# AdaLN layer on one core: the first norm's modulation as columns, three x buffers, one routed sum z per tile, and a new order

## The reference

```python
mod = (silu(c) @ wmod).reshape(4, 6, 1, 256)
sa, ca, ga, sb, cb, gb = mod[:, 0], ..., mod[:, 5]     # ga, gb: sign * max(|.|, 0.25)
h = layernorm(x) * (1 + ca) + sa
x = x + ga * attn(h)        # 16 query heads in 4 groups, d 16, rope, causal softmax over 1024
h = layernorm(x) * (1 + cb) + sb
x = x + gb * ffn(h)
# ffn(h): routed = sigmoid(h @ w_router) > 0.5
#   a = h + (rmsnorm(h, n1) @ wv + bv) @ wo
#   processed = a + (silu(r @ w_gate) * (r @ w_up)) @ w_down, r = rmsnorm(a, n2)
#   where(routed, processed, h)
```

## Time and profile before

| what | value |
|---|---|
| median of 3 runs | 510.67 us (510.49 to 515.2) |
| the profiled execution's own time | 510.83 us |
| its span, first to last instruction | 509.1 us |
| mean granted TensorE clock | 0.970 |
| DMA | 16.07 MB, mean 32 GB/s |

### The profile page before, as it was taken

The page is one execution under the profiler, slowest core; times in us unless marked ns, Lnnn a source line. Parts: engine busy times, 40 slices in busy tenths (PEclk is TensorE's granted clock), DMA queues, the critical chain, the costliest instruction groups (busy, mean ns, idle before and its releaser), DMA issues. The chain is left out here.

```text
span 509.1 us, 9484 instructions
## 1 busy us (share of the span) xinstructions
PE 453.8 (89%) x3308; PEld 376.4 (74%) x3308; DVE 363.1 (71%) x767; ACT 283.4 (56%) x562; POOL 256.9 (50%) x322
## 2 busy tenths in 40 slices
PE   1687879949899999699899999999999999899995
PEld 0266544738887578689887877889888688799995
DVE  4768956599999256989888444899897345847543
ACT  1066437617765684446676477556865766265340
POOL 3270056868414177657541249677524167847234
PEclk9889989968999999989999999999999999989998
DMA  7810101010010010020010010010200001001002
GB/s 226 256 27 1 22 3 42 1 48 0 2 23 1 3 42 1 2 88 2 23 52 2 3 43 1 1 47 23 85 0 8 8 1 43 1 1 42 1 1 84
DMA packets 18353, 16.07 MB, mean 32 GB/s; under 512 B 6265, under 2 KB 16958, under 8 KB 18306
## 3 DMA queue, kind: packets, MB, share of 16 engines
q1 hardware_dynamic: 18306, 15.45, 9.8%
HBM read 11.10 MB, written 4.22 MB: 30 GB/s over the span
## 5 line engine op out<-in xcount | busy, mean ns | idle before, releaser
L761 PE MATMUL banks<-gTh,guhi 128*128 128x256 f32 x352 | 103.2, 293 | 1.7 <-DVE fft L1200 1.5
L862 ACT ACTIVATE PT<-banks 128x1024 f32<-128x1024 f32 (+3 forms) x96 | 75.3, 811 | 43.9 <-PE banks L678 38.5
L763 PE MATMUL banks<-gTh,gulo 128*128 128x256 f32 x352 | 99.1, 282 | 0.0
L762 PE MATMUL banks<-gTl,guhi 128*128 128x256 f32 x352 | 99.1, 282 | 0.0
L761 PEld LDWEIGHTS banks<-gTh,guhi 128*128 128x128 f32 x352 | 66.6, 189 | 6.3 <-issue 4.6
L762 PEld LDWEIGHTS banks<-gTl,guhi 128*128 128x128 f32 x352 | 66.7, 190 | 0.3
L763 PEld LDWEIGHTS banks<-gTh,gulo 128*128 128x128 f32 x352 | 66.7, 189 | 0.0
L1111 DVE TENSOR_REDUCE mxp<-banks 128x2 f32<-128x1024 f32 (+3 forms) x56 | 61.5, 1143 | 6.2 <-PE banks L657 3.0
L516 POOL TENSOR_SCALAR_AFFINE_SELECT PT<-PT 128x512 f32<-128x512 f32 x32 | 21.2, 662 | 66.0 <-ACT PT L862 65.9
L678 PE MATMUL banks<-QKT 128*128 128x512 f32 (+3 forms) x192 | 51.9, 369 | 2.3 <-ACT PT L862 1.3
L652 PE MATMUL banks<-QKT 128*128 128x512 f32 (+3 forms) x192 | 48.8, 364 | 5.8 <-ACT QKT L842 2.1
(11 more groups left out here) (162 smaller groups left out, 1145.7 us busy)
## 6 DMA issues: line engine op xcount, KB each, us to landing
xbuf<-in_L_attn_x SPq DMA_DIRECT2D x8, 512.0 KB, 3.6
out_x<-x SPq DMA_DIRECT2D x8, 512.0 KB, 3.0
wm_st<-in_L_wmod SPq DMA_DIRECT2D x1, 1536.0 KB, 7.3
modB<-mod_scratch SPq DMA_DIRECT2D x4, 256.0 KB, 3.2
wg_st<-in_L_ffn_w_gate SPq DMA_DIRECT2D x1, 704.0 KB, 5.2
wu_st<-in_L_ffn_w_up SPq DMA_DIRECT2D x1, 704.0 KB, 6.3
x<-in_L_ffn_w_down SPq DMA_DIRECT2D x1, 640.0 KB, 5.0
QKT<-mrT SPq DMA_DIRECT2D x32, 4.0 KB
```

The source lines that it names most:

```text
L761: pe.matmul(out_, guhi[:, k, blk, :], gh, start=(m == 0 and k == 0), stop=False)
L762: pe.matmul(out_, guhi[:, k, blk, :], gl, start=False, stop=False)
L763: i = pe.matmul(out_, gulo[:, k, blk, :], gh, start=False, stop=(m == len(blocks) - 1 and k == KB - 1))
L862: act.activation(PT[:, u % 2, 2 * q:2 * q + 2, 0:CH - q0], both("prob", b, n)[:, :, 0:CH - q0], ACT.Exp, scale=float(D) ** -0.5).then_inc( ...
```

## The change

- The shift and scale of the first norm are computed by PE in columns (`pmodc`, [128 x 4] each), for all batches at once, from the first third of wmod, which gets a DMA of its own ahead of x. `vmodc` copies them; `ldA` and its waits are gone. `pmod` multiplies the other four vectors only, and waits for the other two thirds of wmod, whose DMA is issued behind both x chunks and the rope tables.
- DVE keeps the sums over grouped query weights in `setw`; the copies go to ACT (`asetw`), so do the PSUM copies of `amod`, `afwv` and `aw1`; the gates go to POOL (`gmod`), W1's low part too (`gw1`). POOL's zeroing of V, stk and ytm becomes the step `pzero`, and DVE's zeroing of the key tiles the step `vkeys`.
- `xres` holds three batches of x; the residual is added in place. `ldx` of batch 1 has no wait, of batch 2 it waits for the FFN weights' preparation, of batch 3 for a store of batch 0.
- `route` gets a third operation: z = hbuf + dl * routed. `ms2` and `h2` read z; `had`, `hsel` and `zad` are gone; `sum` adds down * routed to z in place; `fin` is z *= gate, x += z. z is a ring of three pairs (`Z_PAIRS`), and `route` waits for the `fin` of three pairs before. `h2` writes into `hbuf`, so `norm2` waits for `h2T`.
- `ORDER` is another table throughout.

The diff, cut to its core (of the two tables only the first lines):

```diff
 LN_EPS, RMS_EPS = 1e-5, 1e-6
-V_CSL, V_SETW, V_MOD, V_FWVT = 2, 3, 8, 9
+V_CSL, V_SETW, V_MODC = 2, 3, 4
+M_SETW, M_MOD, M_FWVT, M_W1 = 1, 2, 3, 4
+C_IDENT, C_ZERO = 3, 5
...
+Z_PAIRS = 3
...
-                 norm2=NJ, hlo=NJ, route=NT, hsel=NT, h2lo=NJ, fft=NJ * NG, fflo=NJ * (NG - 1), sum=NT)
-POOL_STEPS = dict(rstd1=NC, norm1=NT, pmask=ND, rstd2=NJ, hmod=NJ, rs1=NJ, had=NJ, zad=NJ, rs2=NJ, ffl=NJ, fin=NJ)
-SP_STEPS = dict(ldx=NC, ldA=1, ldW=1, ldB=1, ldG=1, mrd=NC, store=NC)
-S_STEPS = dict(setw=1, vmod=1, vprep0=1, vprep1=1, pmod=1, pprep0=1, pprep1=1, aprep=PIECES, awd=1, gprep=PIECES, gwd=1)
+                 norm2=NJ, hlo=NJ, route=NT, h2lo=NJ, fft=NJ * NG, fflo=NJ * (NG - 1), sum=NT)
+POOL_STEPS = dict(rstd1=NC, norm1=NT, pmask=ND, rstd2=NJ, hmod=NJ, rs1=NJ, rs2=NJ, ffl=NJ, fin=NJ)
+SP_STEPS = dict(ldx=NC, ldW=1, ldB=1, ldG=1, mrd=NC, store=NC)
+S_STEPS = dict(setw=1, vmodc=1, asetw=1, amod=1, afwv=1, aw1=1, pmodc=1, pmod=1, pprep0=1, pprep1=1, aprep=PIECES, awd=1,
...
-ldx ldx pmod stats rstd1 norm1 norm1 xT4 setw vmod pprep0 vprep0 pprep1 stats norm1 norm1 xT3 aprep aprep aprep ldA
-wts xev qkv4 xev bias5 qkv3 aprep vprep1 gprep gprep rstd1 norm1 norm1 norm1 norm1 xT2 xT0 gprep ldB xev qkv2 xev
...
+ldx ldx pzero stats rstd1 setw stats pmodc pmod vmodc norm1 norm1 rstd1 norm1 asetw vkeys wts xT4 norm1 xT5 pprep0 xev
+qkv4 xev bias6 amod afwv qkv5 norm1 norm1 norm1 norm1 xT7 xT3 xev aprep gmod ldB ldG ldG ldW qkv7 xev biasq qkvb qkvb
+rope sthi stlo qkvb aprep pprep1 ldx qkv3 aw1 stack4 stack6 stk stk max4 max0 gw1 qkvb rope mxr mxr sthi stlo max6 mxr
...
-        xbuf = sb("xbuf", [P, NT, C])
-        x1 = sb("x1", [P, 2, NT, C])
-        xn, hbuf, dl, hh = (sb(name, [P, TPC, C]) for name in ("xn", "hbuf", "dl", "hh"))
-        dn = sb("dn", [P, 2, C])
+        xres = sb("xres", [P, NX, NT, C])
+        xn, hbuf = (sb(name, [P, TPC, C]) for name in ("xn", "hbuf"))
+        dl = sb("dl", [P, 2, C])
+
+        zbuf = sb("zbuf", [P, Z_PAIRS, 2, C])
...
-                sp.dma_start(cT[:, k, :], c_in[:, k * P:(k + 1) * P].rearrange("b p -> p b")).then_inc(l_mod, 16)
+                sp.dma_start(cT[:, k, :], c_in[:, k * P:(k + 1) * P].rearrange("b p -> p b")).then_inc(l_c, 16)
+            sp.dma_start(wm_st[:, :, 0:CH], wmod[:, 0:CH].rearrange("(k p) n -> p k n", p=P)).then_inc(l_modc, 16)
             load_x(0, 0)
-            sp.dma_start(wm_st[:], wmod.rearrange("(k p) n -> p k n", p=P)).then_inc(l_mod, 16)
...
+            sp.dma_start(wm_st[:, :, CH:6 * C], wmod[:, CH:6 * C].rearrange("(k p) n -> p k n", p=P)).then_inc(l_mod, 16)
...
-            sp.wait_ge(s_setV, V_MOD)
+            sp.wait_ge(s_gmod, 1)
             sp.dma_start(mod_dram, modr).then_inc(s_modw, 16)
             sp.wait_ge(s_modw, 16)
...
-                if kind == "ldA":
-                    if b > 0:
-                        wait("wts", 0)
-                        wait("biasq", 0)
-                    for v in range(2):
-                        sp.dma_start(modc[:, v, :], mod_dram[bass.ds(b, 1), v * C:(v + 1) * C].rearrange(
-                            "o (k p) -> p (o k)", p=P)).then_inc(s_modA, 16)
-                elif kind == "ldW":
...
-                    wait("x1", (n + 1) * NJ // NC - N["x1"])
+                    if b == NX - 1:
+                        sp.wait_ge(s_setG, weights_split)
+                    elif b >= NX:
+                        sp.wait_ge(s_out[n], 16 * (b - NX + 1))
                     load_x(b, n)
...
+                elif kind == "gmod":
+                    pool.wait_ge(s_setM, M_MOD)
+                    rows = modr.rearrange("b (v n) -> b v n", v=4)
+                    gates = rows[:, 0:4:3, :]
+                    pool.tensor_scalar(rows[:, 2, :], rows[:, 2, :], 1.0, 0.0, ALU.add, ALU.add)
+                    then(pool.tensor_scalar(gsgn, gates, 0.0, 2.0, ALU.is_ge, ALU.mult))
+                    then(pool.tensor_scalar(gsgn, gsgn, -1.0, 0.0, ALU.add, ALU.add))
+                    then(pool.tensor_tensor(gabs, gsgn, gates, ALU.mult))
+                    then(pool.tensor_scalar(gabs, gabs, 0.25, 0.0, ALU.max, ALU.add))
+                    pool.tensor_tensor(gates, gsgn, gabs, ALU.mult).then_inc(s_gmod, 1)
+                elif kind == "gw1":
+                    pool.wait_ge(s_setM, M_W1 + 1)
+                    pool.tensor_tensor(flat(W1lo[:]), flat(w1_st[:]), flat(W1hi[:]).bitcast(F32), ALU.subtract
+                                       ).then_inc(s_w1, 1)
...
-                elif kind == "had":
-                    wait("route", 2 * n + 2)
-                    if n >= 2:
-                        wait("h2T", n - 1)
-                    else:
-                        earlier("h2T", NJ + n - 1)
-                    pool.tensor_tensor(hh[:, ring, :], hbuf[:, ring, :], dl[:, ring, :], ALU.add).then_inc(S["had"], 1)
-                elif kind == "zad":
-                    if n == 0:
-                        pool.wait_ge(s_gate, 16 * b + 16)
-                    wait("hsel", 2 * n + 2)
-                    then(pool.tensor_tensor(hbuf[:, ring, :], hbuf[:, ring, :], over_two(gate_b[:, b % 2, :]), ALU.mult))
-                    pool.tensor_tensor(x1[:, b % 2, two, :], x1[:, b % 2, two, :], hbuf[:, ring, :], ALU.add
-                                       ).then_inc(S["zad"], 1)
...
-                    wait("zad", n + 1)
-                    pool.tensor_tensor(x1[:, b % 2, two, :], x1[:, b % 2, two, :], dn[:], ALU.add
+                    if n == 0:
+                        pool.wait_ge(s_gate[b % 2], 16 * (b // 2) + 16)
+                    z = zbuf[:, (b * NJ + n) % Z_PAIRS]
+                    then(pool.tensor_tensor(z, z, over_two(gate_b[:, b % 2, :]), ALU.mult))
+                    pool.tensor_tensor(xres[:, b % NX, two, :], xres[:, b % NX, two, :], z, ALU.add
                                        ).then_inc(S["fin"], 1)
...
-                if kind == "pmod":
+                if kind == "pmodc":
 
                     pe.wait_ge(s_setV, V_CSL)
-                    for m in range(3):
+                    pe.wait_ge(l_modc, 16)
+                    for m in range(2 * KB):
                         for k in range(KB):
-                            i = pe.matmul(bank(m)[0:B, :], csl[:, k, :], wm_st[:, k, m * CH:(m + 1) * CH],
+                            i = pe.matmul(bank(3)[:, m * B:(m + 1) * B], wm_st[:, k, m * P:(m + 1) * P], csl[:, k, :],
+                                          start=(m == 0 and k == 0), stop=(m == 2 * KB - 1 and k == KB - 1))
+                    i.then_inc(s_setP, 1)
+                elif kind == "pmod":
+
+                    pe.wait_ge(s_setV, V_CSL)
+                    pe.wait_ge(l_mod, 16)
+                    for m in range(2):
+                        for k in range(KB):
+                            i = pe.matmul(bank(m)[0:B, :], csl[:, k, :], wm_st[:, k, (m + 1) * CH:(m + 2) * CH],
                                           start=(k == 0), stop=(k == KB - 1))
                     i.then_inc(s_setP, 1)
                 elif kind == "pprep0":
 
                     pe.wait_ge(l_ffn, 96)
-                    pe.wait_ge(s_const, 3)
...
-                    pe.wait_ge(s_modA, b * 32 + 32)
+                    if b == 0:
+                        pe.wait_ge(s_setV, V_MODC)
+                        pe.wait_ge(s_setM, M_SETW)
...
+                elif kind == "afwv":
+                    act.wait_ge(s_setP, 3)
+                    act.activation(flat(fwvT[:]), bank(3), ACT.Copy).then_inc(s_setM, 1)
+                elif kind == "aw1":
+                    act.wait_ge(s_setP, 4)
+                    for k in range(KB):
+                        act.activation(w1_st[:, k, 0:C], bank(k)[:, 0:C], ACT.Copy, scale=n1col[:, k:k + 1])
+                    act.activation(b1[:], bank(2)[:, 0:C], ACT.Copy).then_inc(s_setM, 1)
+                    act.wait_ge(s_setM, M_W1)
+                    act.activation(W1hi[:], w1_st[:], ACT.Copy).then_inc(s_setM, 1)
...
-                    wait("had", n // 2 + 1)
+                    wait("route", n + 1)
                     over_square(n % 2, "ms2", b * NT + n + 1)
-                    act.activation(sq[:, n % 2, :], hh[:, n % TPC, :], ACT.Square, scale=float(C) ** -0.5,
+                    act.activation(sq[:, n % 2, :], zbuf[:, (b * NJ + n // 2) % Z_PAIRS, n % 2, :], ACT.Square, scale=float(C) ** -0.5,
                                    accum_out=ms[:, 1, n:n + 1]).then_inc(S["ms2"], 1)
...
-                elif kind == "vmod":
-
+                elif kind == "vkeys":
+
+                    dve.memset(QKT[HR:P, 2:2 + H:2, :].bitcast(F32), 0.0)
+                    dve.memset(QKT[0:HR, 3:2 + H:2, :].bitcast(F32), 0.0).then_inc(s_keys, 1)
...
+                    o = bank(3)[:, 0:2 * KB * B].rearrange("p (v k b) -> p v k b", v=2, k=KB)
+                    dve.tensor_copy(modc[:, 0], o[:, 0])
+                    assert setup(dve.tensor_scalar(modc[:, 1], o[:, 1], 1.0, None, ALU.add)) == V_MODC
...
```

(29 more changed lines are left out.)

283 lines of the change are left out of this document (136 added, 147 removed).

## The result

The changed kernel takes 488.7 us in the median of four runs (487.46 to 489.71), the kernel before 510.6 in four runs beside it: a ratio of 0.9545, with a 95% interval of 0.9481 to 0.9609. The forecast was 492.0, with a range of 477 to 508.

What follows compares the result with a forecast made beforehand. PE was taken to bound (busy 453.8 of 509.1 us), DVE in early stretches. Start -7.4, then +0.4, 74 for 91.8, 346 for 339, end +1.3: span 492.6, time 494, less 2 for table loads: 492, range 477 to 508.

Steps and rivals of the forecast that it cites:

- Step 1: Start up to the first qkv's bias on DVE: at 25.1 us instead of 32.53, a gain of 7.4 us.
- Step 2: From the start to batch 0's second mneg: DVE bounds, 39.2 us of its steps become 39.6, loss 0.4 us.
- mark 1: Batch 0's second mneg, seen as its mtT starting on PE: forecast to go from 72.5 to 65.5 us.
- Step 3: From batch 0's second mneg to batch 1's second mneg: 74 us instead of 91.8, as FFN work moves later and holes shrink.
- mark 2: Batch 1's second mneg, seen as its mtT starting on PE: forecast at 139.5 us instead of 164.29.
- Step 4: From batch 1's second mneg to the last sum: 346 us instead of 339, 12.1 us more work less 5 back.
- 5 us back: Late stretch: net gain from fewer POOL operations and a shorter chain, less z's ring; between -5 and +12.
- Step 5: The end, from the last sum to the span's end: 7.1 us instead of 5.8, as fin becomes two chained operations.
- fewer table loads: ACT's loads between exp and silu: 15 instead of 19 in the order, worth 2 us.
- The full packing: Rival, first third: that stretch takes its DVE floor, 64 to 68 us, ending at 479 us; chance 0.15.
- the gain given back: Rival, first third and on to batch 2's second mneg: holes stay and DVE is late, 509 us; chance 0.14.
- The ring that stops DVE: Rival, late stretch: route waiting for fin holds later DVE work and through it PE, 520 us; chance 0.08.

Runs made afterwards that it cites:

- e13: e7 with pmod, pprep0, amod and afwv behind the first three qkvs and vkeys behind the first rope; 486.3 us, ratio 0.9515.
- e7: The changed kernel with gmod behind batch 0's second rope, and the modulation's write and four loads behind batch 1's x loads; 485.3 us, ratio 0.9485.
- e10: The changed kernel's steps in the order of the kernel before, with five z pairs and eight hbuf tiles; 528.2 us, ratio 1.0326.
- e11: The changed kernel with 64 unused bytes a partition ahead of gTh, shifting the FFN's operand buffers; 493.3 us, ratio 0.9657.
- e12: The kernel before with 32 unused bytes a partition ahead of gTh, nothing else changed; 509.0 us, ratio 0.9960.
- e9: The changed kernel with 16 unread POOL sums put right ahead of rs2, waiting for ms2 as rs2 does; 492.6 us, ratio 0.9633.
- e8: The changed kernel with 16 unread POOL sums put right behind rs2, waiting for nothing; 486.3 us, ratio 0.9500.
- e14: e7 with five z pairs, eight hbuf tiles and 64 unused bytes a partition ahead of gTh; 486.8 us, ratio 0.9528.
- e4: The changed kernel with 16 unread POOL sums behind each pair's second route, waiting for it, nobody waiting for them; 509.9 us, ratio 0.9952.

## Why the prediction was right or wrong

**Step 1, the start: right.** pmod started at 16.13 (15.9 said) and took 5.85 us (5.0), the bias came at 25.65 (25.1): 6.9 us gained for 7.4. PE stood still for 6.00 us ahead of pmod, and its eight passes started 0.85 us apart at first and 0.43 at the end; in e13, with PE busy just before, the same eight took 3.60 us, all 0.43 apart, near the 3.4 that the step gave for that case. The profile's granted clock reads 1.00 in both places, so that it was the clock rests on these two paces alone.

**Step 2, to mark 1: wrong; this is the step that failed.** "Loss 0.4; the mark goes from 72.5 to 65.5"; it went to 70.0. The missing term is POOL's: I counted its set-up work by POOL's time alone ("not needed before the first wo"), and used the held DVE only as a gain for norm2. The second rope ends 18.2 us behind the first qkv, 14.4 before. Of these 3.8 us e7 gives back 3.5. With 0.5 us less won in the start (6.9 for 7.4) and 0.6 us more from the rope to the mark (28.5 for 27.9, where I had 0.4 of loss in all) that is the 4.5 us between 65.5 and 70.0. For pprep1, which I put at nothing, e7 leaves 0.3 us of the 3.8.

The kernel before was held too, right ahead of the mark: its mneg took 2.45 us for 0.16 beside POOL's gwd.

```profile
69.65 2.52 DVE L1122 TENSOR_SCALAR mt<-mx 128x8 fp32r<-128x8 f32 x2
```

```profile
68.64 3.43 POOL L497 TENSOR_TENSOR wdlo<-x,wdhi 128x1536 fp32r<-128x1536 f32 x1
```

In the changed kernel these 2.3 us are gone, and 3.9 us of batch 1's statistics stand in the same stretch. e13 shows on what the mark hangs: with the first qkv 6.2 us earlier but the third and fourth only 0.3, the second rope and the mark come 0.3 us earlier.

**Step 3, mark 1 to mark 2: right.** 74.1 us for 74. The holes did close: in 70:100, PE is idle for 1.7 of 30 us and DVE busy for 19.36, and in 100:120 PE is busy for 17.41 us, 12.56 before. e10 shows that the order does this: 90.6 us in the old one. By the prediction's count 9.8 of the 16.5 us between the two are work that the new order does behind mark 2.

**Step 4, the late stretch: right in sign, the term "5 us back" mis-sized.** From mark 2 to the last sum's start 336.8 us, 346 said: 14 us came back where I had 5. The late stretch of the kernel before, in the columns of the earlier trace rows:

```profile
164.29:504.30 340.01, 326.77 (x2522) 282.75 (x2522) 234.21 (x492) 200.97 (x403) 179.08 (x211) 0.99 0.07 21
```

The 86 matmuls more, costed form by form with the durations of the kernel before, are 12.1 us, as the step had it. PE is idle for 8.6 us instead of 13.2, 4.6 less; and the same matmuls keep it busy for 10.3 us less, mostly in gate, up and down (8.5): 340.0 + 12.1 - 4.6 - 10.3 = 337.2. The 4.6 is the 5 that I had. The 10.3 I had not looked for: 1638 FFN matmuls x 2.4 ns = 4.0 us are the pace, which e11 and e12 tie to where new buffers pushed the old ones. The other 6.3 I can only argue for, by a granted clock of 1.00 instead of 0.99.

Of its inner terms: the shorter chain counts (e9: 3 to 6 us), POOL's smaller load doesn't (e8, which puts back 16 of its 32 operations). norm2's mean fell to 569 ns (under 700 said), 5.6 us of the 10.6 over-length, twice what I counted, with no effect on the end that a run shows. The ring's waits, r_yes on fin in the changed kernel, are 3.7 us in two places, and e14 shows that even these cost nothing.

**Step 5, the end: right.** 6.6 us from the last sum's start (7.1 said), and 16 table loads. What fewer table loads are worth, put at 2 us, no run shows.

Put together: mark 2 was 4.6 us later than said, the late stretch 9.2 shorter, the end 0.5 shorter, and the 2 us for table loads were counted apart: 492.0 + 4.6 - 9.2 - 0.5 + 2.0 = 488.9. Two errors of some size lay on opposite sides: that the forecast came within 3.3 us is partly luck.

**The rivals.** The full packing (479) and the gain given back (509) did not come. The ring that stops DVE did not come either; but its mechanism, an engine in order that holds ready work behind one wait, is what made e4 slower by 21 us, on POOL in place of DVE. Of what would have shown me wrong nothing came. Of the signs for being right, POOL's busy time (225.8 us, 220 said) and the first qkv (23.4) came as said, mark 1 (70.0 for about 65) didn't, and mark 2 was 4 us late.

## What to carry to other kernels

Work moved to an engine with time to spare has three prices that its busy time doesn't show: what stands behind it there in order (gmod ahead of norm1 in e10), what it waits for while others stand behind it (62.6 us in e4), and whether it holds a neighbour's operation (0.41 us became 3.24). Where an order written by hand goes with new steps, neither has a worth by itself: from mark 1 on the new steps brought some 2 us in the old order, and one operation a pair put back into the new order cost 21 to 27 where it waits for route, and nothing behind rs2. Before a difference of a per cent is put down to a step, compare the pace of the untouched matmuls: an edit that only moves buffers can make 5 us.

## What the runs showed of the hardware that I had not expected

- The same fp32r matmuls, nearly all 128x256, start every 116.2 to 116.6 ns in eight builds and every 118.8 to 119.6 in four, with two between them (116.8 and 117.2), and 64 or 32 unused bytes a partition move a build from one to the other. In the changed kernel whole gate, up and down steps run at 113 to 115 ns and others at 118; neither the PSUM bank nor the slot of gTh tells them apart, and why is open.
- A DVE operation was held over two POOL instructions in a row: it started at 36.38, before gw1 at 36.55, and ended at 39.62, 0.29 us after the first of gprep's two ended. In e7 the same two instructions held a tensor_scalar of 0.16 us for 2.27.
- A POOL operation on 4 partitions costs as much as on 128: tensor_tensor 1.26 us for 4x512 (1.27 for 128x516), tensor_scalar 1.93 to 2.12 for 4x512.
